# Layer 0's low parts made by an adding DMA in place of a subtraction on POOL

## The reference

```
# layer 0; adj holds 0 or 1 here, so only kind 1 (a0) can be chosen
e0    = leaky(einsum('bid,bjd->bij', h * a0[:, 0], h))
alpha = sigmoid(where(adj == 1, e0, -max))
x     = layernorm(x + einsum('bij,bjd->bid', alpha, h) + bias)
# layer 1
Hh = h @ W ;  s = Hh @ a_src ;  d = Hh @ a_dst
e  = where(adj != 0, exp(-leaky(s_i + d_j)), 0)
x  = layernorm(x + elu((e @ Hh) / rowsum(e)))
```

## Time and profile before

| | |
|---|---|
| median of 3 runs | 1378.3 us (1376.89 to 1379.58) |
| the profiled execution | 1379.31 us, span in the profile 1377.5 us |
| busy share of PE, DVE, ACT, POOL | 93%, 75%, 62%, 61% |
| granted TensorE clock, mean | 0.99 |
| one graph in the steady loop | 82.5 us (the same instruction at 641.15 us and again 82.5 us later) |

### The profile page before, as it was taken

The page is one execution under the profiler, slowest core; times in us unless marked ns, Lnnn a source line. Parts: engine busy times, 40 slices in busy tenths (PEclk is TensorE's granted clock), DMA queues, the critical chain, the costliest instruction groups (busy, mean ns, idle before and its releaser), DMA issues.

```text
span 1377.5 us, 27394 instructions
## 1 busy us (share of the span) xinstructions
PE 1277.8 (93%) x7874; PEld 1142.0 (83%) x7874; DVE 1030.4 (75%) x2594; ACT 855.3 (62%) x2129; POOL 841.3 (61%) x1228
## 2 busy tenths in 40 slices
PE   3899999999999999999999999999999998999986
PEld 3788888888888888988888888888888888888875
DVE  3677878777787777778777787877778777787864
ACT  3665757567574765757567574765757567574642
POOL 4465838557394765838567394765838567394732
PEclk9999999999999999999999999999999999999998
DMA  6344251623406143251623406143250623406001
GB/s 142 61 77 101 40 103 47 110 72 63 109 11 126 57 82 97 42 105 40 110 72 65 107 16 121 57 86 93 45 109 32 110 72 65 107 15 122 27 5 33
DMA packets 190352, 101.73 MB, mean 74 GB/s; under 512 B 140656, under 2 KB 173808, under 8 KB 190320
## 3 DMA queue, kind: packets, MB, share of 16 engines
q1 hardware_dynamic: 171888, 67.79, 20.9%
q0 software_dynamic: 18432, 33.56, 14.5%
HBM read 84.55 MB, written 16.78 MB: 74 GB/s over the span
## 4 chain that ended last, share of the span: by engine, by line
PE 39%; POOL 24%; DVE 19%; issue 11%; ACT 5%; DMA 1%; DVEq 0%; POOLq 0%; SPq 0%; ACTq 0%
POOL coef_lo L368 13%; PE acc_bank L1207 11%; PE hh_bank L1186 5%; DVE coef L867 5%; PE acc_bank L1088 4%; PE acc_bank L1090 4%; PE acc_bank L1089 4%; PE lg_bank L1088 3%; PE lg_bank L1090 3%; PE lg_bank L1089 3%; POOL var_eps L376 3%; POOL rstd L379 2%; POOL rstd L389 2%; DVE stats L907 2%; DVE reluP L902 2%
## 5 line engine op out<-in xcount | busy, mean ns | idle before, releaser
L1207 PE MATMUL acc_bank<-H,coef 128*128 128x258 f32 x2048 | 468.9, 383 | 10.4 <-ACT reluP L607 9.1
L1207 PEld LDWEIGHTS acc_bank<-H,coef 128*128 128x128 f32 x2048 | 382.7, 190 | 72.1 <-issue 18.1
L368 POOL TENSOR_TENSOR coef_lo<-coef,coef_hi 128x1024 fp32r<-128x1024 f32 x128 | 306.0, 2392 | 77.4 <-ACT coef_hi L553 75.6
L1088 PE MATMUL acc_bank<-h_hi,coef_hi 128*128 128x256 f32 x1024 | 297.9, 291 | 1.8 <-issue 1.8
L1090 PE MATMUL acc_bank<-h_hi,coef_lo 128*128 128x256 f32 x1024 | 286.9, 280 | 0.0
L1089 PE MATMUL acc_bank<-h_lo,coef_hi 128*128 128x256 f32 x1024 | 286.8, 280 | 0.0
L867 DVE SCALAR_TENSOR_TENSOR coef<-tr_bank,E_col,codeT 128x256 f32<-128x256 f32 x512 | 209.1, 476 | 39.3 <-PE acc_bank L1207 36.8
L1088 PEld LDWEIGHTS acc_bank<-h_hi,coef_hi 128*128 128x128 f32 x1024 | 195.2, 191 | 2.9 <-issue 2.0
L1089 PEld LDWEIGHTS acc_bank<-h_lo,coef_hi 128*128 128x128 f32 x1024 | 195.8, 191 | 0.0
L1090 PEld LDWEIGHTS acc_bank<-h_hi,coef_lo 128*128 128x128 f32 x1024 | 195.5, 191 | 0.0
L553 ACT ACTIVATE coef_hi<-coef 128x1024 fp32r<-128x1024 f32 x128 | 135.6, 1060 | 86.5 <-DVE coef L806 86.1
(11 more groups left out here) (76 smaller groups left out, 2280.3 us busy)
## 6 DMA issues: line engine op xcount, KB each, us to landing
code_nat<-in_adj POOLq DMA_DIRECT2D x128, 256.0 KB, 5.0
x_raw<-in_x SPq DMA_DIRECT2D x16, 1024.0 KB, 5.6
out<-x SPq DMA_DIRECT2D x128, 128.0 KB, 1.7
codeT<-code_nat SPq DMA_TRANSPOSE x128, 3.3
W_ext<-in_L_gnn_W SPq DMA_DIRECT2D x1, 256.0 KB, 2.8
score<-in_L_gnn_a SPq DMA_DIRECT2D x1, 256.0 KB, 6.8
bias_bc<-in_L_gnn_bias SPq DMA_DIRECT2D x1, 128.0 KB, 3.5
a_col<-in_L_gnn_a SPq DMA_DIRECT2D x4, 1.0 KB, 2.1
```

The lines of the kernel that those rows point to most:

```text
L368: nc.gpsimd.tensor_tensor(coef_lo[:, t % 4, :, :], blocks(coef[:, t % 4, :]), f32(coef_hi[:, t % 4, :, :]), ALU.subtract).then_inc(S.lo0, 1)
L1088: nc.tensor.matmul(dst, lhs_hi, rhs_hi, start=first, stop=False)
L1207: ins = nc.tensor.matmul(acc_bank[t % 2][:, 0:HC], coef[:, SLOT1[t], J * P:(J + 1) * P], H[:, J, :], start=J == 0, stop=J == NT - 1)
```

## The change

ACT now makes a second pass over the masked tile and writes its negated rounding into `coef_lo`; only then does it signal `hi0`. POOL no longer computes: it issues a DMA which adds `coef` (512 KB) onto what stands in `coef_lo`. PE and DVE wait for that DMA's completion, with one semaphore for each of the four buffers in place of one counter.

```
@@ -63,7 +63,7 @@
             self.codes_turned = [sem(tag + f"codes_turned{i}") for i in range(8)]
         self.mask0 = sem(tag + "mask0")
         self.hi0 = sem(tag + "hi0")
-        self.lo0 = sem(tag + "lo0")
+        self.lo0 = sem(tag + "lo0") if general else [sem(tag + f"lo0_{i}") for i in range(4)]
         self.agg0 = sem(tag + "agg0")
         self.resid0 = sem(tag + "resid0")
         self.stats0 = sem(tag + "stats0")
@@ -242,6 +242,7 @@
 
         dve_past = sem("dve_past")
         sp_past = sem("sp_past")
+        pool_past = sem("pool_past")
         flag_step = sem("flag_step")
         flag_summed = sem("flag_summed")
         flag_ready = sem("flag_ready")
@@ -365,8 +366,13 @@
             def low0(S, b, t):
 
                 pool.wait_ge(S.hi0, NT * b + t + 1)
-                nc.gpsimd.tensor_tensor(coef_lo[:, t % 4, :, :], blocks(coef[:, t % 4, :]),
-                                        f32(coef_hi[:, t % 4, :, :]), ALU.subtract).then_inc(S.lo0, 1)
+                if S is F:
+                    pool.sem_inc(pool_past, 1)
+                    pool.dma_start(f32(coef_lo[:, t % 4, :, :]), blocks(coef[:, t % 4, :]),
+                                   accum_op=ALU.add).then_inc(F.lo0[t % 4], 16)
+                else:
+                    nc.gpsimd.tensor_tensor(coef_lo[:, t % 4, :, :], blocks(coef[:, t % 4, :]),
+                                            f32(coef_hi[:, t % 4, :, :]), ALU.subtract).then_inc(GEN.lo0, 1)
 
 
 
@@ -550,8 +556,11 @@
                     act.wait_ge(S.agg0, NT * b + t - 3)
                 elif prev:
                     act.wait_ge(S.agg0, NT * b + t - 3)
-                nc.scalar.activation(coef_hi[:, t % 4, :, :], blocks(coef[:, t % 4, :]),
-                                     ACT.Copy).then_inc(S.hi0, 1)
+                ins = nc.scalar.activation(coef_hi[:, t % 4, :, :], blocks(coef[:, t % 4, :]), ACT.Copy)
+                if S is F:
+                    ins = nc.scalar.activation(coef_lo[:, t % 4, :, :], blocks(coef[:, t % 4, :]), ACT.Copy,
+                                               scale=-1.0)
+                ins.then_inc(S.hi0, 1)
 
 
 
@@ -787,7 +796,7 @@
                 dve.wait_ge(F.tanh, NT * b + t + 1)
                 dve.wait_ge(F.codes_turned[t], 16 * b + 16)
                 if t >= 4:
-                    dve.wait_ge(F.lo0, NT * b + t - 3)
+                    dve.wait_ge(F.lo0[t % 4], 32 * b + 16)
                 elif prev:
                     dve.wait_ge(F.agg1, NT * b + t - 5)
                 for m, (tt, j0, j1) in enumerate(MIRRORS):
@@ -858,7 +867,8 @@
                 if t == 0 and prev:
                     dve.wait_ge(F.agg1, NT * b)
                 elif 2 <= t < 6:
-                    dve.wait_ge(F.lo0, NT * b + t + 4)
+                    for i in range(2):
+                        dve.wait_ge(F.lo0[t - 2 + i], 32 * b + 32)
                 elif t == 6:
                     dve.wait_ge(F.agg1, NT * b + 2)
                 at = SLOT1[t]
@@ -1142,7 +1152,10 @@
 
             def aggregate0(S, b, t, prev):
 
-                pe.wait_ge(S.lo0, NT * b + t + 1)
+                if S is F:
+                    pe.wait_ge(F.lo0[t % 4], 32 * b + 16 * (t // 4) + 16)
+                else:
+                    pe.wait_ge(GEN.lo0, NT * b + t + 1)
                 if t == 0:
                     pe.wait_ge(S.h_lo, 4 * b + 4)
```

## The result

The changed kernel took 1393.1 us in the median of 4 runs (1391.5 to 1395.9), the kernel before 1378.9 us (1376.9 to 1381.0) beside it. The ratio is 1.0105, interval 1.0082 to 1.0128. The profiled execution has a span of 1391.7 us, 14.2 us above that of before. The forecast was 1391 us.

A forecast was written before the change was run, and what follows sets the result against it. POOL held 24% of the chain, but ACT was to become the bound after the change. 1379.3 + 11.1 (loop) + 3.8 (start) - 2.5 (last graph) = 1391.7, so 1391 us for the median, range 1370 to 1435.

The forecast's parts named there:

- ACT's second pass, 0.97 us: ACT's queue: each added scaled pass takes 0.97 us, bounded by 0.95 and 1.06; those of rounds 2 to 4 do not hide.
- The room, 1.30 us: ACT's idle time from 641.15 to `x1T` of tile 3, 1.30 us against 2.91 for three passes, leaving ACT 1.61 late.
- `hT_lo`, +1.41: DVE, round 5: `low_xT` waits for ACT's late `gT_hi` and begins 1.41 us later, at 658.45 instead of 657.04.
- `norm0(4)`, 0.40 us as before: DVE, behind `low_xT` of round 5: moves from 658.43 to 659.84 and is done 0.40 us later.
- the slack of 0.67: PE at tile 4: the tile was ready 0.67 us before its transposes, so PE begins only 0.74 us later.
- PE no longer waits for `norm0(1)` to `(3)`; it waits for `x1T` instead: PE, tiles 1 to 3: waits for DVE `x` fall from 42.9 below 20 us, those for `x1T` rise over 20.
- DVE's mask, 0.65 us a block: DVE's mask: a block of 512 takes 0.65 us without POOL's subtraction, with no cost or gain on the path.
- The DMA: POOL's adding DMA: issue 0.6 us, landing 5.0 to 5.6 with the issue, hidden with about 0.6 to spare.
- Start, +3.8: Kernel start, once: the first product waits for ACT's second pass and the DMA in place of the subtraction, +3.8 us.
- POOL's relief reaches PE: Rival, chance 0.15: ACT fits after all and PE loses its waits for `norm0`, 1339 to 1375 us.
- The DMA lands late: Rival, chance 0.25: landing over 6.2 us from the signal makes PE stand at tile 2, 1400 to 1454 us.

The follow-up runs named there:

- the DMA alone: The changed kernel without ACT's second pass, so the adding DMA adds onto zeros, then sums, and low parts are wrong: 1361.3 us, ratio 0.9891.
- `high0` first: The changed kernel with ACT's two `high0` passes ahead of `watch_codes` in each round instead of behind it: 1389.6 us, ratio 1.0089.
- two DMAs: The changed kernel with a second 512 KB DMA, from `coef` to spare HBM, issued on the same queue ahead of each adding one: 1416.8 us, ratio 1.0288.
- the pass alone: The kernel before with ACT's second pass added and POOL still subtracting over its result: 1454.2 us, ratio 1.0565.
- the run without the DMA: The changed kernel with POOL only giving the signal in place of the adding DMA, low parts wrong: 1379.5 us, ratio 1.0021.

## Why the prediction was right, step by step

The direction, the mechanism (ACT becomes the bound of rounds 2 to 4, the DMA is hidden in the loop) and the time held: 1391 against 1393. Of the terms, some were off and made up for each other. In spans: loop +14.6 (15 x 0.975; predicted 11.1), start +2.6 (predicted 3.8), from the last `x1T` of tile 0 to the end -3.0 (predicted -2.5), 14.2 in all. So the loop cost 3.5 us more than I had and the two ends 1.7 less, and in the loop one term was too large and one too small: that the sum came within 2 us is partly luck.

- **ACT's second pass, 0.97 us.** Right: 653.74 to 654.69 is 0.95, and ACT runs without a gap.
- **The room, 1.30 us.** Off by 0.3: I summed the idle time that the rows flag. ACT came out 1.29 us late, and 3 x 0.95 = 2.85, so the room was 1.56. A row that waits for nothing begins about 0.1 us ahead of the recorded end of the one before it, as 654.69 does against 653.74 + 1.07; a wait also takes this overlap away, so removing it frees more than its flag.
- **`hT_lo`, +1.41.** It came +1.11 (the wait 1.39 us long, `ACT gT_hi` as its releaser): the same 0.3.
- **`norm0(4)`, 0.40 us as before.** This is the step that failed: in 11 of 15 graphs it took 0.82 to 0.84 beside POOL's `xb`, 0.43 more. In those graphs its end moved by 1.54, with about 0.1 more to PE's start, less the slack of 0.67, which is 0.97 where I had 0.74: from `x1T` of tile 0 to PE's transposes of tile 4 it is 19.37 us (651.14 to 670.51), and was 18.40 (641.15 to 659.55). In the other four it is 18.94, 0.54 more than before, which is my 0.74 less the 0.3 of the room and with that 0.1 added. The mean of the 15 is 0.86; the remaining 0.12 us a graph stand outside this stretch and are not traced. PE's wait for `reluP` grew by 2.0 us in all (9.1 before), but it is 11.1 in the run with the DMA alone too, so ACT's second pass is not its cause.

  I had put POOL's relief at no cost, without asking what moving POOL's other instructions would bring beside DVE's. The trace of before had the answer, in `norm0(1)` with `xb` beside it:

```profile
643.27 0.72 POOL L363 TENSOR_TENSOR xb<-x_raw,bias_bc 128x256 f32<-128x256 f32 x1
643.33 0.80 DVE L836 TENSOR_SCALAR x<-resid,moments,rstd 128x256 f32<-128x256 f32 x1 [0.44 <-POOL rstd L379]
```

  The run with one `next_bias` moved confirms it.
- **"PE no longer waits for `norm0(1)` to `(3)`; it waits for `x1T` instead."** Wrong: 48.6 us in 61 waits, not under 20, and `hh_bank` for `x1T` 2.1, not over 20. POOL's power starts 0.26 us sooner behind the high part, not over 1 us, because the second pass and the DMA's issue stand in the subtraction's place. This moved the place of the idle time and not its end, since ACT ran without a gap either way: `high0` first shows the waits where I had put them, at a time 2 us lower.
- **DVE's mask, 0.65 us a block.** Right: 0.68 for one block of 512 and 1.29 for two. The gain lies where the subtraction had stood beside the mask: at tile 5 (a block of 512 and one of 256) it took 2.27 us before, at 640.62, and 1.00 now, at 649.71.

```profile
642.42 0.68 DVE L815 SCALAR_TENSOR_TENSOR coef<-score,codeT 128x512 f32<-128x512 f32 x1
...
661.41 1.29 DVE L815 SCALAR_TENSOR_TENSOR coef<-score,codeT 128x512 f32<-128x512 f32 x2
```

- **The DMA.** Its issue takes 0.89 us, not 0.6 (within 0.53 to 1.1). Its landing is 4.7 us, not 5.0 to 5.6:

```profile
L371 POOL DMA_DIRECT2D coef_lo<-coef x128: 850/891/942, 50.3 to 1330.6; - x128
...
DMA to landing us min/median/max: 4.5/4.7/7.4
```

  No wait of PE in the loop names it. At tile 2 the issue stood at 641.82 and PE began at 647.68 + 0.14, so 1.3 us were to spare where I had 0.6. The Trainium skill, page "SBUF — State Buffer", section "SBUF: two separate sides", says that VectorE, while an instruction of it holds the ports that the two share, can keep GpSimd from writing a DMA's descriptors. Here 128 issues stayed between 0.85 and 0.94 us and the fastest and the median landing lie 0.2 us apart, so no stall of that kind is seen. The long landings are few: the first four DMAs, issued 1.9 us apart, landed after 4.6, 5.6, 6.4 and 7.4 us, and in the loop none took more than 5.8. The 5.7 us that the DMA did cost in the loop are no landing: its issue moved POOL's `xb` beside `norm0(4)`.
- **Start, +3.8.** The first product moved from 51.08 to 54.97, +3.9, as forecast. But `x1T` of tile 0 came only 2.6 us later (by the one trace of each; runs that are the same up to there differ by over 1 us). PE made the products up to there without a wait in both kernels, 12.15 us before and 10.83 now; before, its granted clock was 0.50 from 51.08 to 57.0 us, now from 54.97 to 58.1. I had no term for the clock; why it stayed low for longer before is open.
- **The rival "POOL's relief reaches PE"**: without the second pass it does, but with 15 us (the DMA alone), not the 39 that removing all waits would have given. **"The DMA lands late"**: it did not, with 1.3 us to spare at tile 2; in the run with two DMAs, where the low part came 2.6 us later, PE did wait for it.

Open: the 1.6 us of the last graph that the DMA costs are measured as a difference and not traced to a row.

## What to carry to other kernels

Relieving an engine that holds a share of the chain helps only as far as its signal comes sooner: add up from the same first instruction (here the high part) to the signal that others need (the power), before and after; 2.39 us less work had become 0.26 us. Moving work onto another engine is paid for round by round in the stretch where that engine has the least room, so first clear that stretch, by moving what is not needed there: here such moves were worth 19 to 40 us, and decided whether the change itself lost 14 us or won 7. When an instruction of POOL moves, look at what it comes to stand beside on DVE, and look at more than one graph: a collision can stand in some of them only.

## What the runs showed of the hardware

- A `TENSOR_SCALAR` of 128x256 on DVE took 0.40 to 0.41 us alone and 0.80 to 0.84 beside POOL's `TENSOR_TENSOR` of 128x256. Both times shown here it ended 0.14 to 0.15 us behind the end of POOL's: 669.53 + 0.84 against this row, and 643.33 + 0.80 against 643.27 + 0.72 before.

```profile
669.49 0.73 POOL L364 TENSOR_TENSOR xb<-x_raw,bias_bc 128x256 f32<-128x256 f32 x1
```

  The mask's 1.46 us beside the subtraction and 0.68 without it is the same picture: it ended at 633.88, the subtraction (from 630.94, 2.39 us) at 633.33. By the Trainium skill, page "SBUF — State Buffer", section "SBUF: two separate sides", VectorE and GpSimd share a pair of ports exclusively: an instruction of VectorE that uses it (in a mode of two ports, or with two inputs in SBUF) is blocked until one of GpSimd that started first is done. Both observations agree.
- An adding DMA of 512 KB within SBUF landed 4.7 us after its issue (the median) and took 0.89 us on POOL's queue, against 0.57 for a plain load.
- TensorE, after 3.24 us of idleness in the run with the pass alone, showed a granted clock of 0.54 from 680 to 685 us, nearly all of it at the level of 1.2 GHz, and the products of 128x256 started 0.22 us apart (679.89, 680.11); in the whole run PE was busy 1307.7 us for the work that took 1279.2 in the changed kernel. The changed kernel's first products, behind 5.53 us of idleness, took 0.41 us too, and so did those of the kernel before behind 1.76 us, where they took 0.28 behind 0.42 us of idleness in the run without the DMA.
